# Layer 0's feed-forward: codes expanded inside its main block, layer 1's first weights and x prepared in its last ticks

## The reference, cut to what matters

```python
x = L0_attn_x
xn = _layernorm(x)
s = _L0_attn_ref(xn, ...)                 # linear attention with decay
g = _silu(_L0_ffn_ref(xn, w_fc, w_proj))  # this stage
x = x + s * g
xn = _layernorm(x)
s = _L1_attn_ref(xn, wq, wk, wv, wo)      # softmax attention with rope
g = _silu(_L1_ffn_ref(xn, ...))
x = x + s * g

def ternarize_weights(w):
    gamma = mean(abs(w))
    return sign(round(w / (gamma + EPS))) * gamma
def bitlinear(x, w):       # layer_norm, absmax_quant, then x_hat @ w_hat.T
```

## Time and profile before

| | us |
|---|---|
| median of 3 runs | 3008.83 |
| lowest, highest | 3008.29, 3011.52 |
| the profiled execution | 3014.07 |
| span of its records | 3012.3 |
| PE busy | 2851.8 (95%) |
| DVE / ACT / POOL busy | 1857.4 / 1292.5 / 1412.6 |

### The profile page before, as it was taken

The page is one execution under the profiler, slowest core; times in us unless marked ns, Lnnn a source line. Parts: engine busy times, 40 slices in busy tenths (PEclk is TensorE's granted clock), DMA queues, the critical chain, the costliest instruction groups (busy, mean ns, idle before and its releaser), DMA issues. The chain is left out here.

```text
span 3012.3 us, 54363 instructions
## 1 busy us (share of the span) xinstructions
PE 2851.8 (95%) x19392; PEld 2012.1 (67%) x19392; DVE 1857.4 (62%) x2724; ACT 1292.5 (43%) x2021; POOL 1412.6 (47%) x1000
## 2 busy tenths in 40 slices
...
DMA packets 124567, 238.99 MB, mean 79 GB/s; under 512 B 13440, under 2 KB 48384, under 8 KB 124416
## 3 DMA queue, kind: packets, MB, share of 16 engines
...
## 5 line engine op out<-in xcount | busy, mean ns | idle before, releaser
L1286 DVE TENSOR_REDUCE l_attn_maxima<-l_attn_ps_max 128x2 f32<-128x1024 f32 x502 | 613.2, 1222 | 234.9 <-PE l_attn_ps_max L1414 230.8
L1257 POOL TENSOR_TENSOR l_attn_summed<-l_attn_summed,l_attn_probs 128x1024 f32<-128x1024 f32 x248 | 585.8, 2397 | 51.2 <-ACT l_attn_probs L1195 51.2
L1195 ACT ACTIVATE l_attn_probs<-l_attn_ps_sc 128x1024 f32<-128x1024 f32 x512 | 497.6, 1029 | 158.0 <-PE l_attn_ps_sc L1402 131.2
L1257 POOL TENSOR_TENSOR l_attn_summed<-l_attn_probs 128x1024 f32<-128x1024 f32 x124 | 293.7, 2391 | 241.5 <-ACT l_attn_probs L1195 241.5
L1662 POOL TENSOR_TENSOR l_ffn_ht_lo<-l_ffn_mixed,l_ffn_ht_hi 128x512 fp32r<-128x512 f32 x88 | 114.0, 1296 | 414.2 <-ACT l_ffn_ht_hi L1683 414.2
L62 PE MATMUL l_attn_ps_prep<-l_w_tile,l_x_tiles 128*128 (+1 forms) x1440 | 286.1, 347 | 6.4 <-DVE l_attn_qk_lo L1280 2.1
L1424 PE MATMUL l_attn_ps_y<-l_attn_probs,l_attn_v 128*32 128x512 f32 x2048 | 273.2, 606 | 1.1 <-ACT l_attn_probs L1195 1.1
L62 PEld LDWEIGHTS l_attn_ps_prep<-l_w_tile,l_x_tiles 128*128 128x128 f32 x1440 | 247.8, 189 | 39.0 <-issue 29.1
L71 PE MATMUL l_ffn_ps_fc<-l_ffn_t_fc,l_ffn_ct_hi 128*128 128x512 f32 x512 | 213.4, 417 | 7.0 <-DVE l_ffn_ct_lo L823 3.6
L71 PE MATMUL l_ffn_ps_out<-l_ffn_t_proj,l_ffn_ht_hi 128*128 128x512 f32 x512 | 206.1, 402 | 0.0
L71 PE MATMUL l_ffn_ps_fc<-l_ffn_t_fc,l_ffn_ct_lo 128*128 128x512 f32 x512 | 203.8, 398 | 0.0
...
## 6 DMA issues: line engine op xcount, KB each, us to landing
...
```

Source lines behind the costliest of these rows:

```text
L1195: act.activation(probs[kt % RING][:, hs, :], ps_sc[:, hs, :], ACT.Exp, scale=ATT_SCALE).then_inc(exp_done, 1)
L1257: pool.tensor_tensor(total[:, hs, :], old[:, hs, :], probs[kt % RING][:, hs, :], ALU.add).then_inc(added, 1)
L1286: dve.tensor_reduce(maxima[b][:, j, PAIR * hp:PAIR * hp + PAIR, half:half + 1], pair, AX.X, ALU.max).then_inc(max_read, 1)
```

## The change

1. The block that only expanded the codes is gone. At the start of the main block DVE expands pieces 0 and 1 of `t_fc` and ACT pieces 2 and 3; POOL writes the constants and `half_gamma`. `t_proj` is expanded later: two pieces on POOL at its tick -1, two on ACT between the Gelus of tick 0. TensorE waits for the four pieces of `t_fc` before tick 0 and for those of `t_proj` before tick 2, and ACT waits for `t_proj` before the first `hc`.
2. In tick 32 (CHUNKS) SP waits for the last `squares`, then loads the four pieces of layer 1's group 0 into the tile `squares` and four chunks of x into `x_tiles`. At the end of tick 33 ACT makes `w_hi` and DVE `w_lo` of group 0. Layer 1's block no longer does these steps; TensorE there waits for the constants alone before its first matmul.
3. For that the tiles of layer 0's feed-forward and of layer 1 share memory: `t_fc`, `ct_hi`, `ct_lo` and `xt1` lie in `w_tile`, `probs` and some tiles of `layer1_ffn` lie in `stage`. `w_tile` is laid out by group, then by k. The counts of `xt_ld` are smaller by one load, and ACT waits once for the three later groups of weights.

```diff
 def layer0_ffn(...)
-        t_fc = sb("t_fc", [P, KD, FC], F32R)
+        t_fc = w_tile[:, 0:KD * FC].rearrange("p (k n) -> p k n", k=KD)
...
-        with ExitStack() as prep:
-            made = prep.enter_context(nc.semaphore("l0_ffn_made"))
-            block = prep.enter_context(nc.Block())
...
-            @block.scalar
-            def _(act):
-                for k in range(KD):
-                    act.activation(t_fc[:, k, :], fc_codes[:, k, :], ACT.Copy)
-
-            @block.vector
-            def _(dve):
-                dve.tensor_scalar(half_gamma[:, :], gamma_w[:, 1:2], 0.5 * FC ** 0.5, None, ALU.mult)
-                for k in range(0, KF, KF // KD):
-                    dve.tensor_copy(t_proj[:, k:k + KF // KD, :], proj_codes[:, k:k + KF // KD, :])
...
+            def next_stage():
+                w_in = wqkvT.rearrange("(k p) g n -> p k g n", p=P)
+                sp.wait_ge(squared, CHUNKS)
+                for k in range(KD):
+                    sp.dma_start(raw[:, k, :], w_in[:, k, 0, :]).then_inc(raw_in, 16)
+                for b in range(2):
+                    sp.wait_ge(xt_stored[b], 32)
+                for c in range(CHUNKS // CPB):
+                    sp.dma_start(fp32(x_tiles[:, c, :, :, :]).rearrange("p h k n -> p (h k n)"), xt_out[c]).then_inc(x_ahead, 16)
+
             def tick(t, p):
+                if isinstance(t, int) and t == CHUNKS:
+                    next_stage()
                 c, b = t + 4, p
...
+            def expand(n):
+                pool.tensor_copy(t_proj[:, PIECE * n:PIECE * (n + 1), :], proj_codes[:, PIECE * n:PIECE * (n + 1), :]).then_inc(proj_expanded, 1)
+
             def tick(t, p):
+                if isinstance(t, int) and t == -1:
+                    expand(2)
+                    expand(3)
...
         @block.scalar
+            def prologue():
+                for k in (2, 3):
+                    act.activation(t_fc[:, k, :], fc_codes[:, k, :], ACT.Copy).then_inc(fc_expanded, 1)
...
+            def next_weights():
+                act.wait_ge(fc_done, NF * CHUNKS)
+                act.wait_ge(raw_in, 16 * KD)
+                for k in range(KD):
+                    act.activation(w_hi[:, k, :], raw[:, k, :], ACT.Copy).then_inc(w_hi_made, 1)
...
+                        if isinstance(t, int) and t == 0 and n < 2:
+                            expand(n)
...
+                    if isinstance(t, int) and t == 0:
+                        act.wait_ge(proj_expanded, KD)
                     act.activation(hc[p][:, :], h[p][:, :], ACT.Identity, ...)
...
         @block.vector
+            def prologue():
+                for k in (0, 1):
+                    dve.tensor_copy(t_fc[:, k, :], fc_codes[:, k, :]).then_inc(fc_expanded, 1)
+
+            def next_weights():
+                for k in range(KD):
+                    dve.wait_ge(w_hi_made, k + 1)
+                    dve.tensor_tensor(w_lo[:, k, :], raw[:, k, :], fp32(w_hi[:, k, :]), ALU.subtract)
...
         @block.tensor
+                if isinstance(t, int) and t == -1:
+                    pe.wait_ge(made, CONSTANTS)
+                if isinstance(t, int) and t == 0:
+                    pe.wait_ge(fc_expanded, KD)
+                if isinstance(t, int) and t == 2:
+                    pe.wait_ge(proj_expanded, KD)
...
 def layer1_attention(...)
-                sp.dma_start(raw(0)[:, 0, :], w_in[:, 0, 0, :]).then_inc(raw_in[0], 16)
-                load(0, 0)
-                for k in range(1, KD):
-                    sp.dma_start(raw(0)[:, k, :], w_in[:, k, 0, :]).then_inc(raw_in[k], 16)
-                for c in range(1, CPB):
+                for c in range(XTS, CPB):
                     load(0, c)
...
-                for k in range(KD):
-                    act.wait_ge(raw_in[k], 16)
-                    act.activation(w_hi[:, k, 0, :], raw(0)[:, k, :], ACT.Copy).then_inc(w_hi_made, 1)
...
+                act.wait_ge(later_in, 16 * (GROUPS - 1))
                 split(1)
...
-                for k in range(KD):
-                    dve.wait_ge(w_hi_made, k + 1)
-                    dve.tensor_tensor(w_lo[:, k, 0, :], raw(0)[:, k, :], fp32(w_hi[:, k, 0, :]), ALU.subtract).then_inc(w_lo_made, 1)
...
                 pe.wait_ge(made, CONSTANTS)
-                pe.wait_ge(w_lo_made, KD)
```

More of the change, by code:

```diff
@@ L557, in layer0_ffn @@
         sem = lambda name: ctx.enter_context(nc.semaphore(f"l0_ffn_{name}"))
-        t_fc = sb("t_fc", [P, KD, FC], F32R)
+        t_fc = w_tile[:, 0:KD * FC].rearrange("p (k n) -> p k n", k=KD)
+        w_hi, w_lo = (w_tile[:, KD * 3 * DIM * i:KD * 3 * DIM * i + KD * 3 * P].rearrange("p (k n) -> p k n", k=KD) for i in range(2))
         t_proj = sb("t_proj", [P, KF, DIM], F32R)
@@ L597, in layer0_ffn @@
         codes = two("codes", [P, DIM])
-        ct_hi, ct_lo = two("ct_hi", [P, KD, P], F32R), two("ct_lo", [P, KD, P], F32R)
+        small = lambda first, count: [w_tile[:, KD * FC + DIM * (first + i):KD * FC + DIM * (first + i + 1)].rearrange("p (k n) -> p k n", k=KD) for i in range(count)]
+        ct_hi, ct_lo = small(0, 2), small(2, 2)
         h = [stage[:, FC * i:FC * (i + 1)] for i in range(2)]
@@ L606, in layer0_ffn @@
         xn1 = two("xn1", [P, DIM])
-        xt1 = two("xt1", [P, 2, KD, P], F32R)
+        xt1 = [w_tile[:, KD * FC + DIM * (4 + 2 * i):KD * FC + DIM * (6 + 2 * i)].rearrange("p (h k n) -> p h k n", h=2, k=KD) for i in range(2)]
         st_a, st_f = two("st_a", [P, 6]), two("st_f", [P, 6])
@@ L901, in layer1_attention @@
         sem = lambda name: ctx.enter_context(nc.semaphore(f"l1_attn_{name}"))
[L902 removed]
+        w_hi, w_lo = (w_tile[:, KD * 3 * DIM * i:KD * 3 * DIM * (i + 1)].rearrange("p (g k n) -> p k g n", k=KD, g=GROUPS) for i in range(2))
         cos_t, sin_t = sb("cos_t", [P, CPB, R]), sb("sin_t", [P, CPB, R])
@@ L1130, in _ @@
                 sp.wait_ge(y_den_stored[b], 32 * NT)
-            sp.wait_ge(x_ahead, 16 * CHUNKS // CPB)
+            for b in range(XTS):
+                sp.wait_ge(xt_ld[b], 16 * (CPB // XTS) * NT)
         @block.scalar
@@ L1557, in layer1_ffn @@
         sc_gate, sc_up, sc_down = sb("sc_gate", [P, KH]), sb("sc_up", [P, KH]), sb("sc_down", [P, DIM])
-        yt, den = two("yt", [P, GROUPS, P]), two("den", [P, GROUPS, P])
+        yt, den = [stage[:, DIM * (14 + i):DIM * (15 + i)].rearrange("p (g n) -> p g n", g=GROUPS) for i in range(2)], two("den", [P, GROUPS, P])
         xt_ld = sem("xt_ld")
```

85 lines of the change are left out of this document (48 added, 37 removed).

## The result

| | before | after |
|---|---|---|
| median, us (7 runs each) | 3011.72 | 3000.89 |
| lowest, highest | 3008.29, 3014.58 | 2999.1, 3003.27 |
| ratio, 95% interval | | 0.9965 [0.9953, 0.9977] |
| span of the profiled execution | 3012.3 | 2997.8 |

The change gains 10.5 us (6.9 to 14.2). Forecast were 11.6 us and 2997.2; the kernel before itself was 2.9 us slower here than in the three runs that the forecast was set against.

A forecast was written before the change was run, and what follows sets the result against it. PE, busy 95%, was taken to lose time in two barrier waits, 17.6 and 12.2 us. Terms -7.6 + 0.9 + 0 + 0 - 4.9 = -11.6 us gave 2997.2 from 3008.83; own range 2995.1 to 3000.7, stated range 2993.5 to 3004.6.

The forecast's parts named there:

- Head of layer 0's feed-forward, -7.6: Before layer 0's feed-forward: x loads issued at attention's barrier start the chain from `bn_stats` to TensorE 7.6 us earlier.
- POOL's casts, +0.9: Layer 0's feed-forward head: POOL's two casts hold DVE's `xnn` of chunk 1, delay 0.9 us, bounds 0 and 8.3.
- X: Time of one POOL cast of 128x2048 in layer 0's feed-forward head, taken as 2.0 us; 3 in the range's slow end.
- the row of equal size: Profile row of a one-input POOL operation with the same 2048 columns, 2.0 us, used for the cast time.
- the row of the tensor_scalar: POOL's tensor_scalar, 2.86 us for 1024 columns, so 5.7 per cast; rival total 3004.6 us, chance 0.12.
- 2X - 3.1: Formula for the delay of `xnn` of chunk 1 behind POOL's two casts, never below zero; 0.9 us.
- The row at 267.56: DVE tensor_scalar that took 0.54 us in the middle of a POOL operation; by it the casts' delay would be none.
- Tick 0 and the last ticks, 0: Layer 0's feed-forward: ACT's expansions in tick 0, tick 32's loads and tick 33's weight preparation are hidden, costing 0.
- 0 to 5: Tick 32: microseconds to spare before POOL's mix of chunk 30 needs its loads; slow-queue rival 3008.5 us, chance 0.06.
- Head of layer 1's attention, -4.9: Layer 1's first product: TensorE waits only for POOL's constants, not the last `w_lo`, and starts 4.9 us earlier.
- the clock ... stays so; up to 1.2 us: After layer 1's head gap: TensorE's lower clock was expected to stay as before, up to 1.2 us either way.
- an effect that the trace before can't show: Anywhere in the kernel: unseen effects such as the tiles' new places, given no size, chance 0.02.

The follow-up runs named there:

- after_again: The changed kernel as it is, measured and traced again beside three others on one chip: 3001.5 us, ratio 0.9961 to the kernel before.
- dve_casts: The changed kernel with POOL's two casts of `t_proj` given to DVE's idle stretch in tick 0: 3001.39 us, ratio 0.9953 to the kernel before.
- places_only: The kernel before with only `t_fc`, `ct_hi`, `ct_lo` and `xt1` placed in one tile, in the changed kernel's order: 3010.75 us, ratio 0.9992.
- l1_only: The changed kernel with layer 0's feed-forward given back its own block for the codes, new places kept: 3006.9 us, ratio 0.998 to before.

## Why the prediction was right or wrong

**Head of layer 0's feed-forward, -7.6.** Right. What hides DVE's two casts is the load, the prediction said, with 0.4 us to spare. In `after` the casts end last (no idle time ahead of `bn_stats`, which starts 2.36 us after the first cast), in `after_again` the load does by 0.68 us, in `dve_casts` by 0.40. This varies by some 0.7 us between traces and moves the head as much: from the first cast to the first matmul with `t_fc` are 11.7 us in `after` and 12.4 in `after_again`.

**POOL's casts, +0.9.** X was taken as 2.0 from the row of equal size and is 1.98 on average (1.89 and 2.08); the row of the tensor_scalar would have misled. The delay is 0.70 us from `bn_stats` to the first matmul: 0.54 by the casts (`dve_casts`), 0.16 by the third load of x, which comes a little later. What failed is a part of the mechanism: DVE does not wait "until POOL is done" but until POOL's running instruction is. With two casts and two tensor_scalar operations this comes to the same moment, 0.28 us behind the second cast, which is why 2X - 3.1 fitted; with four casts it was wrong by 3.4 us. That it fitted was in part luck. The sum left out the hold of `codes` of chunk 0, which the prediction names as issued beside the casts. By its own words `codes` would have stood until both casts were done, at 596.5 instead of 593.1; less the 1.0 us that DVE idles behind it before the third `bn_stats`, that is an estimate of 2.4 us and not 0.9. The measured hold of `codes` was 1.09 us, which DVE would have spent waiting for the third load of x, and `xnn` had to sit out the second cast anyway. The row at 267.56, from which the prediction drew a delay of none, was one exception among 16 such pairs of the trace before.

**Tick 0 and the last ticks, 0.** Right. The two ACT expansions stand between the first Gelus, and DVE still idles 7.06 us for the fourth Gelu. The queue had 6.1 us to spare, 1.5 of them from the longer tick that the prediction didn't have; the other 4.6 are near the upper end of its 0 to 5, the one worked out from the full rate. Tick 0 is 0.6 us shorter (0.3 in `after_again`), since the clock rises 3.8 us after the first matmul (4.6) instead of 5.0: 11.3 to 12.2 us over all the traces, inside the 1.2 us allowed.

**Head of layer 1's attention, -4.9.** Right at the place, 7.73 to 2.81 us. Mis-sized is what follows, "the clock ... stays so; up to 1.2 us". From the first product to the third rounding of the maxima (`max_t`) are 135.6 us before and 138.7 after. In seven traces with the changed head it is 137.5 to 138.9 (mean 138.0), in five with the old one 132.6 to 138.1 (mean 135.5). The clock accounts for the difference: in this stretch TensorE was granted 1.2 GHz for 43.8 us on average in the seven and for 38.9 in the five, and if each such microsecond is counted as half a lost one, an estimate, what is left is 116.1 and 116.0 us. In the pair of traces compared above it shows in the first 30 us:

```profile
1194.00:1209.00 15.00, 15.00 (x80) 14.52 (x80) 5.69 (x22) 3.75 (x12) 0.00 (x0) 0.91 0.67 234
1209.00:1224.00 15.00, 12.49 (x65) 9.47 (x64) 13.46 (x25) 2.75 (x8) 0.00 (x0) 0.89 0.67 255
```

```profile
1177.80:1192.80 15.00, 15.00 (x77) 14.70 (x78) 5.38 (x21) 3.43 (x12) 0.00 (x0) 0.86 0.49 171
1192.80:1207.80 15.00, 12.56 (x60) 9.49 (x59) 13.59 (x23) 3.06 (x9) 0.00 (x0) 0.83 0.71 266
```

(before first, then after). The mean over those 30 us is 0.84 in all seven with the changed head and 0.84, 0.85, 0.90, 0.90 and 0.95 in the five with the old one. So about half of the 4.9 us is on average given back within 136 us, twice the 1.2 us that the prediction allowed at this place. The five with the old head differ by 5.5 us among themselves, so the size is not settled; with the wait moved, one trace has 132.7 and the other 137.2.

**What no term covered.** The tiles' places: -1.84 us in the loop, +1.54 us by the clock behind it. The prediction had them as 0.02 for "an effect that the trace before can't show". They cancel but for 0.3 us, which is luck.

The sum of the parts, by pairs of traces from the first expansion to the first product of layer 1 (615.07 us before, 614.12 in `places_only`, 608.88 in `l1_only`, 602.75 and 601.68 in `after_again` and `after`): places -0.9, second half -5.2, first half -6.1 and -7.2, then on the mean +2.5 behind that product: -10 to -11. The forecast had the two halves, 11.6 us against 11.3 to 12.4; it lacked the first of these terms and had the last only as up to 1.2 us either way. One slip in its range has no effect: X = 3 and 1.2 us of clock add 3.2 us to -11.6, not 3.5.
